# An mLSTM and ternary feed-forward layer: the opening's gates in one group, two value units of sequence 1 moved, two sums on another engine

## The reference

```python
x = x + mlstm(layernorm(x), Wq, Wk, Wv, Wog, Wig, big, Wfg, bfg, gamma, Wout)
x = x + ffn(layernorm(x), w1, b1, w2, b2)

# mlstm, 8 heads, key width 32, value width 64; i and f: gate rows (8 x 512 each)
i, f = 15*tanh((x @ Wig.T + big)/15), 15*tanh((x @ Wfg.T + bfg)/15)
# per step: m = max(logsig(f)+m, i); C = F*C + I*k v^T; n = F*n + I*k
# h = (q C) / (max(|q n|, exp(-m)) + eps); norm per head * gamma
# out = (sigmoid(x @ Wog.T) * h) @ Wout.T

# ffn: w1q, w2q = sign(w) * (|w| >= 0.7*mean|w|)      (2048 wide)
# out = gelu(x @ w1q.T + b1) @ w2q.T + b2
```

## Time and profile before

| | us |
|---|---|
| median of 3 runs | 1740.55 (1740.52 to 1741.01) |
| the profiled execution | 1742.3 |
| its span in the profile | 1740.6 |
| TensorE busy | 1707.5 (98%) |
| VectorE busy | 1437.6 (83%) |
| ScalarE busy | 1059.6 (61%) |

### The profile page before, as it was taken

One profiled execution on the slowest core, in us unless ns is written; L12 is line 12 of the kernel. 1 busy time (PEld: TensorE's weight loads), 2 busy tenths in 40 slices (PEclk: granted clock), 3 DMA queues, 4 the chain that ended last, 5 costly groups with the idle time before them and its releaser, 6 DMA issues.

```text
span 1740.6 us, 31380 instructions
## 1 busy us (share of the span) xinstructions
PE 1707.5 (98%) x12028; PEld 841.4 (48%) x12028; DVE 1437.6 (83%) x2528; ACT 1059.6 (61%) x1769; POOL 606.6 (35%) x477
## 2 busy tenths in 40 slices
PE   6899999999999999999999999999999999999999
PEld 4554445444444444445444444444444444454455
DVE  7888788897888978789887888988789788886872
ACT  6978375473746638375573746648375573847643
POOL 1242514335241442514235241442514235241430
PEclk9999999999999999999999999999999999999999
DMA  8736253442725326253442725336262442625120
GB/s 321 219 89 167 58 141 72 117 120 56 170 60 127 87 80 160 58 154 59 120 117 56 171 60 126 87 92 152 55 161 61 110 119 56 148 59 132 33 55 25
DMA packets 294981, 187.45 MB, mean 108 GB/s; under 512 B 239136, under 2 KB 260640, under 8 KB 289712
## 3 DMA queue, kind: packets, MB, share of 16 engines
q1 hardware_dynamic: 293248, 182.30, 41.7%
q10 hardware_dynamic: 1584, 3.15, 0.5%
HBM read 96.47 MB, written 20.23 MB: 67 GB/s over the span
## 4 chain that ended last, share of the span: by engine, by line
PE 81%; DVE 8%; DMA 3%; SPq 3%; issue 2%; POOL 1%; ACT 1%; POOLq 0%; DVEq 0%; ACTq 0%
PE pf L2073 24%; PE pf L2057 22%; PE pa L1926 17%; PE pa L1902 7%; PE psh L1926 5%; SPq L530 2%; PE psh L2013 2%; DMA kT<-shared 1%; PE psh L1968 1%; PE psh L2047 1%; DVE gT L1633 1%; PE pa L2013 1%; DVE dec L1482 1%; PE pa L1893 1%; PE psh L2009 1%
## 5 line engine op out<-in xcount | busy, mean ns | idle before, releaser
L2073 PE MATMUL pf<-w2T,gT 128*128 128x512 f16 x2048 | 505.8, 379 | 0.0
L2057 PE MATMUL pf<-x2T,w1T 128*128 128x512 f16 x1920 | 422.0, 379 | 0.0
L2057 PEld LDWEIGHTS pf<-x2T,w1T 128*128 128x128 f16 x1920 | 185.4, 98 | 222.5
L2073 PEld LDWEIGHTS pf<-w2T,gT 128*128 128x128 f16 x2048 | 195.5, 97 | 177.0
L1633 DVE SCALAR_TENSOR_TENSOR gT<-g,wscale,gT 128x512 f16<-128x512 f32 x240 | 208.5, 871 | 22.5 <-ACT gT L1046 20.2
L1926 PE MATMUL pa<-wT,xT 128*128 128x512 f16 x960 | 212.8, 379 | 0.6 <-ACT sig L970 0.6
L1043 ACT ACTIVATE g<-pf,b1c 128x512 f32<-128x512 f32 x240 | 164.1, 684 | 72.5 <-PE pf L2057 56.6
L1046 ACT ACTIVATE gT<-g,wscale 128x512 f16<-128x512 f32 x240 | 173.3, 722 | 7.9
L1926 PE MATMUL pa<-wT,shared 128*128 128x512 f16 x768 | 176.2, 379 | 1.6 <-DMA shared<-qT 0.8
L1051 ACT ACTIVATE ktok<-kT 128x512 f32<-128x512 f32 x64 | 40.4, 631 | 216.4 <-DVE kT L1528 214.9
L1902 PE MATMUL pa<-xT,wT 128*128 128x512 f16 x768 | 171.4, 379 | 0.0
(11 more groups left out here) (246 smaller groups left out, 2705.2 us busy)
## 6 DMA issues: line engine op xcount, KB each, us to landing
dec<-gate_r SPq DMA_DIRECT2D x32, 1024.0 KB, 6.1
xin<-L_attn_x SPq DMA_DIRECT2D x16, 1024.0 KB, 6.0
out<-x1b SPq DMA_DIRECT2D x64, 256.0 KB, 2.3
xres<-L_attn_x SPq DMA_DIRECT2D x16, 512.0 KB, 4.3
xres<-L_attn_x SPq DMA_DIRECT2D x32, 256.0 KB, 3.0
qw<-gate_w SPq DMA_DIRECT2D x128, 48.0 KB, 2.0
s<-state_w SPq DMA_DIRECT2D x60, 97.5 KB, 2.4
qw<-kT SPq DMA_DIRECT2D x120, 48.0 KB, 2.0
```

Source lines behind the costliest of these rows:

```text
L2057: last = nc.tensor.matmul(bank, w1T[:, k, tok(f)], x2T[:, part, :, k, :], start=(k == 0 and part == HI), stop=(k == KD - 1 and part == LO))
L2073: last = nc.tensor.matmul(bank, gT[:, part, f, tok(t)], w2T[:, f, :], start=(f == 0 and part == HI), stop=(f == NF - 1 and part == LO), sk ...
```

## The change

Everything that changes is in the first 135 us of the run.

- ScalarE loads its table by a small square at the very start; the squares of the query and key weights go behind the value and gate weights.
- The transposes and sums of `maxima` are parted, so that other work can stand between them.
- The gates of sequence 0 go to one column group (`first_gates`): all twelve matmuls add into the same 32 rows. ScalarE takes tanh directly from the bank, then the absolute value, then the exponential (`first_exponents`); the copy and the three additions are gone for this sequence. On VectorE the gate weights' lower part comes before two of the value weights, and the logarithm's steps stand apart (`gate_one`, `gate_rest`), ahead of `sequence(0)`.
- ScalarE's w2 sums: 0 ahead of tanh, 1 behind it, 2 and 3 behind the keys (before: 0, 1 and 2 ahead of tanh, 3 behind the keys).
- The w1 sums of pairs 2 and 3 become one reduction on VectorE (`absolute_sums(1)`), between `norm_apply(1)` and `chunk_decay(0)`.
- Two of the query weights' transposes go behind value tile 0 on TensorE.
- Value tile 1 of sequence 1 goes to the second bank of `pf`, in the place of 18 idle matmuls, of which 5 stay; ScalarE reads it between ternary pairs (pair 9 is taken earlier). Tiles 2 and 3 go ahead of projections 2 and 3 of sequence 0.

```diff
 s_dchain = sem("s_dchain")
+s_table = sem("s_table")
 s_sums = sem("s_sums")
...
 s_wfree = [sem(f"s_wfree{n}") for n in range(6)]
-s_abs = sem("s_abs")
+s_abs, s_abs_dve = sem("s_abs"), sem("s_abs_dve")
 s_asum = sem("s_asum")
...
-    sums = Chain(0, 4 + UNITS // 2)
+    sums = Chain(0, 4 + UNITS // 2 - 2)
...
+        act.wait_ge(gate_dve, at(b, 4, 0))
+        nc.scalar.activation(ge, ge, ACT.Exp).then_inc(gate_act, 1)
+    def gate_log(b):
         act.wait_ge(gate_dve, at(b, 4, 1))
-        nc.scalar.activation(ge, ge, ACT.Exp).then_inc(gate_act, 1)
-    def gate_log(b):
+        nc.scalar.activation(gl, gu, ACT.Ln).then_inc(gate_act, 1)
+    def gate_floor(b):
         act.wait_ge(gate_dve, at(b, 4, 2))
-        nc.scalar.activation(gl, gu, ACT.Ln).then_inc(gate_act, 1)
-    def gate_floor(b):
+        nc.scalar.activation(stack[32:32 + NH, :], gu, ACT.Exp, scale=-1.0).then_inc(gate_act, 1)
+    def late_decays(b):
         act.wait_ge(gate_dve, at(b, 4, 3))
-        nc.scalar.activation(stack[32:32 + NH, :], gu, ACT.Exp, scale=-1.0).then_inc(gate_act, 1)
-    def late_decays(b):
-        act.wait_ge(gate_dve, at(b, 4, 4))
         if b > 0:
...
         gate_log(b)
-        value(b, 1)
+        if not (isinstance(b, int) and b == 1):
+            value(b, 1)
         value(b, 2)
...
+    def first_exponents():
+        bank = pa_bank(0, U_GATE)
+        act.wait_ge(pa_fill, pa_filled(0, U_GATE))
+        nc.scalar.activation(th, pa[0:GROWS, bank, :], ACT.Tanh, bias=gate_bias[:, 0:1],
+                             scale=evac[0:GROWS, W_GATE:W_GATE + 1]).then_inc(tanh_ok, 1)
+        act.wait_ge(tanh_ok, 1)
+        nc.scalar.activation(ge, th[0:NH, :], ACT.Abs).then_inc(pa_free[bank], 1)
+        act.wait_ge(pa_free[bank], pa_done(0, U_GATE))
+        nc.scalar.activation(ge, ge, ACT.Exp, scale=-CAP).then_inc(gate_act, 1)
     def opening():
-        gate_copy(0)
-        absolute_sums2(1, 2)
-        gate_tanh(0)
+        absolute_sums2(0)
+        first_exponents()
+        absolute_sums2(1)
         value(0, 0)
-        gate_exp(0)
-        absolute_sums1(6, early=True)
+        gate_log(0)
         weights_hi(*USES_QK[0:3])
...
         weights_hi(USES_QK[3])
-        gate_log(0)
+        replace_rows(G_QK)
+        absolute_sums1(6, early=True)
         value(0, 2)
-        replace_rows(G_QK)
         weights_hi(*USES_O[0:2])
+        gate_floor(0)
         value(0, 3)
-        gate_floor(0)
         act.wait_ge(s_abs, sums.n)
...
         keys(0, 1)
-        absolute_sums2(3)
         weights_hi(USES_O[3])
+        absolute_sums2(2)
         replace_rows(G_O)
...
         gate_columns(0)
-        absolute_sums1(7, 0)
+        absolute_sums2(3)
         queries(0, 1)
-        absolute_sums1(1, 2, 3)
+        absolute_sums1(7, 0, 1)
         output_gate(0, 0)
...
             act.wait_ge(ps_fill, at(b, PS_FILLS, F_V + 1))
-            bank, free = ps[:, 1, :], ps_free[1]
+            bank, free = pf[:, 1, :] if isinstance(b, int) and b == 1 else ps[:, 1, :], ps_free[1]
         else:
...
             small2_gone(12)
+            ternary_out(9)
         squares(b, 2)
...
         if not run_f:
-            ternary_out(9)
+            value(1, 1)
             small2_gone(13)
...
+    act.wait_ge(s_pchain, 1)
+    nc.scalar.activation(hinv[:, :], half[:, :], ACT.Square).then_inc(s_table, 1)
     sum_squares(G_V)
     sum_squares(None)
-    sum_squares(G_QK)
     split_hi(*range(KD))
...
     replace_rows(G_V)
-    absolute_sums2(0)
+    sum_squares(G_QK)
     sequence(0, None, True)
...
-    def bounds(cols, step):
+    def row_maxima(step):
...
                                 ALU.mult).then_inc(s_rowmax, 1)
+    def bounds(cols, step):
+        known = PEAK_COLS[step - 1]
+        n = known.stop - known.start
         dve.wait_ge(s_allmax, step)
...
+    def absolute_sums(n):
+        dve.wait_ge(s_w12[0][n], 16)
+        nc.vector.tensor_reduce(asum1[:, 2 * n:2 * n + 2],
+                                rows[:, 4 * n:4 * n + 4, :].rearrange("p (n u) d -> p n (u d)", u=2), AX.X, ALU.add,
+                                apply_absolute_value=True).then_inc(s_abs_dve, 1)
     def thresholds():
-        dve.wait_ge(s_abs, 4 + UNITS // 2)
+        dve.wait_ge(s_abs, 4 + UNITS // 2 - 2)
+        dve.wait_ge(s_abs_dve, 1)
         nc.vector.tensor_reduce(asums[:, 0:1], asum1[:, :], AX.X, ALU.add)
...
         bank = pa_bank(b, U_GATE)
-        dve.wait_ge(gate_lo, at(b, 1, 1))
+        dve.wait_ge(gate_lo, at(b, 1, 0))
         nc.vector.tensor_tensor(th, pa[2 * QUAD:2 * QUAD + GROWS, bank, :], th, ALU.add).then_inc(gate_part, 1)
-        dve.wait_ge(gate_part, at(b, 2, 1))
+        dve.wait_ge(gate_part, at(b, 2, -1))
         nc.vector.tensor_tensor(th, pa[QUAD:QUAD + GROWS, bank, :], th, ALU.add).then_inc(gate_part, 1)
-        dve.wait_ge(gate_part, at(b, 2, 2))
+        dve.wait_ge(gate_part, at(b, 2, 0))
         nc.vector.tensor_tensor(th, pa[0:GROWS, bank, :], th, ALU.add).then_inc(pa_free[bank], 1)
...
         nc.vector.tensor_scalar(ge, th[0:NH, :], CAP, None, ALU.mult).then_inc(gate_arg, 1)
-        dve.wait_ge(gate_arg, at(b, 3, 1))
+        dve.wait_ge(gate_arg, at(b, 3, 0))
         nc.vector.scalar_tensor_tensor(ge, ge, -1.0, ge, ALU.mult, ALU.min).then_inc(gate_dve, 1)
+    def first_floor():
+        dve.wait_ge(tanh_ok, 1)
+        nc.vector.tensor_scalar(gf, th[0:NH, :], CAP, 0.0, ALU.mult, ALU.min)
     def gate_logs(b):
...
         nc.vector.tensor_scalar(gf, th[0:NH, :], CAP, 0.0, ALU.mult, ALU.min)
-        if b == 0:
-            scales(LATER, 2)
+        gate_one(b)
+        gate_rest(b)
+    def gate_one(b):
...
         nc.vector.tensor_scalar(gu, ge, 1.0, None, ALU.add).then_inc(gate_dve, 1)
-        if b == 0:
-            weights_lo(USES_QK[0])
-        dve.wait_ge(gate_dve, at(b, 4, 2))
+    def gate_rest(b):
+        dve.wait_ge(gate_dve, at(b, 4, 1))
         nc.vector.scalar_tensor_tensor(ge, gu, 1.0, ge, ALU.subtract, ALU.subtract).then_inc(gate_arg, 1)
-        dve.wait_ge(gate_arg, at(b, 3, 2))
+        dve.wait_ge(gate_arg, at(b, 3, 1))
         nc.vector.tensor_tensor(gf, gf, ge, ALU.add).then_inc(gate_arg, 1)
...
-        if b == 0:
-            gate_minus(b)
-            gate_logs(b)
-            weights_lo(*USES_QK[1:4])
         dve.wait_ge(i_loaded, at(b, 16, 16))
         nc.vector.tensor_scalar(gi, gi, CAP, None, ALU.mult)
-        dve.wait_ge(gate_arg, at(b, 3, 3))
+        dve.wait_ge(gate_arg, at(b, 3, 2))
         dve.wait_ge(gate_act, at(b, 5, 2))
...
             norm_apply(b + 1, range(T))
+            absolute_sums(1)
             chunk_decay(b)
...
     norm_apply(0, range(T))
+    row_maxima(1)
     bounds(EARLY, 1)
...
     split_lo(2, 3)
-    weights_lo(*USES_V)
+    weights_lo(*USES_V[0:2])
     weights_lo(USE_GATE)
+    weights_lo(*USES_V[2:4])
     largest()
-    gate_sum(0)
+    first_floor()
+    row_maxima(2)
+    gate_one(0)
     bounds(LATER, 2)
+    gate_rest(0)
+    scales(LATER, 2)
+    weights_lo(*USES_QK)
     sequence(0, None, True)
...
-    def maxima(sums, peak_count, step):
+    def peak_transpose(sums, peak_count, step):
...
         nc.tensor.transpose(peak_rows[0:n, :], peak[:, known], ident[:, :]).then_inc(s_rows, 1)
+    def peak_sums(step):
+        n = PEAK_COLS[step - 1].stop - PEAK_COLS[step - 1].start
         pe.wait_ge(s_rowmax, step)
...
             pe.wait_ge(xT_loaded, at(b, 16, -16))
+    def first_gates():
+        bank = take_pa(0, U_GATE)
+        for k in range(KD):
+            for n, (ws, xs) in enumerate(PARTS):
+                last = nc.tensor.matmul(bank[0:QUAD, :], wgT[:, k, ws, :], xT[:, xs, :, k, :],
+                                        start=(k == 0 and n == 0), stop=(k == KD - 1 and n == 2))
+        last.then_inc(pa_fill, 1)
...
             opening()
-        else:
+        elif not (isinstance(b, int) and b == 1):
             late_values(b, 2)
...
         weights_ready(USE_GATE)
-        gates(0)
-        weights(*USES_QK[0:2])
+        first_gates()
         weights_ready(*USES_V)
         tokens(0, U_V, xT[:, :, 0, :, :], C_V)
-        maxima(3, 1, 2)
-        weights(USES_QK[2])
+        peak_transpose(3, 1, 2)
+        weights(USES_QK[0])
+        peak_sums(2)
+        weights(*USES_QK[1:3])
         late_values(0, 1)
...
         weights_out(2, 3)
-        busy_until(10, 18)
+        pe.wait_ge(pf_free[0], 5)
+        keep_busy(pf[:, 0, :], 5)
+        x_ready(1)
+        pe.wait_ge(ps_free[1], at(1, PS_USES[1], 0))
+        pe.wait_ge(pf_free[1], 5)
+        token_products(pf[:, 1, :], xT[:, :, 1, :, :], C_V).then_inc(ps_fill, 1)
+        ternary_transpose(10)
+        pe.wait_ge(ps_free[1], at(1, PS_USES[1], 1))
         ternary_transpose(11)
...
         ternary_transpose(13)
-        x_ready(1)
         gates(1)
...
         ternary_transpose(15)
-        late_values(1, 1)
         tokens(1, U_V, xT[:, :, 0, :, :], C_V)
+        late_values(1, 2)
+        late_values(1, 3)
         project(0, 2)
```

(11 more changed lines are left out.)

## The result

The changed kernel takes 1744.03 us (median of 20 runs, 1741.64 to 1747.01), the kernel before 1740.53 (20 runs, 1739.36 to 1741.91): ratio 1.0021, 95% interval 1.0014 to 1.0027. It is slower, by 3.5 us where 1.65 was forecast, and outside the range (1737.3 to 1743.6). Its runs also spread more: standard deviation 1.57 us against 0.63. Its profiled execution took 1741.64, the shortest of its runs, and that of before 1742.3, above all 20 of its timed runs. The two spans (1739.9 and 1740.6) rank the kernels the wrong way round, so the stretches have to be compared. Up to the first feed-forward use of sequence 1 (144.75 before, 145.53 after) the changed kernel is 0.78 us later. From there to the end it is 1595.9 us before and 1594.4 after; over all 18 traces of this document this rest takes 1594.1 to 1596.6 us, so it differs between executions by more than the change is worth.

A forecast was written before the change was run, and what follows sets the result against it. TensorE, 98% busy, was taken as the bound. Opening 0, VectorE sum and order +0.2, projection 3 +1.83, old slack -0.38 gave +1.65 us on 1740.55: 1742.2 us; 8-in-10 range 1737.3 to 1743.6.

The forecast's parts named there:

- Items 1 and 2: Opening: earlier tanh and one gate group; gate matmuls at 20.9, V0 at 25.5, first keys about 0.6 us later.
- Item 3: Opening: keys 0.6 us late are hidden in TensorE's 1.14 us wait at 46.06 for a lower weight part.
- Item 4: Opening: gate rows, issued earlier, still queue behind sequence 1's x and land at 39.2 to 39.5; gain 0.
- Item 5: Opening: the w1 reduction moved to VectorE delays chunk decays, thresholds and ternary products by 0.2 us.
- The handover order: Sequence 0 to 1: keys start 3.35 us earlier, but projection 3 ends 1.83 us later, delaying work that waits for it.
- All three waits: Handover: TensorE idles ahead of sequence 1's first query, gate transposes and second query, using up the 3.35 us.
- The full gain: Rival: keys start 3.35 us earlier and nothing behind stops TensorE, giving 1737.2 us; chance 0.17.
- the cancelling: Rival: projection 3's lateness costs only 0.25 at the gate transposes, giving 1740.8; chance 0.18 together with gate rows passing the loads.
- the end of the fourth score product: Behind the handover: it ends at 157.9, before TensorE wants the bank at 158.6, so its lateness hides.
- the 3.35 us are waited away in three places, and TensorE goes on 1.65 us later: Handover: three waits consume the earlier keys; the second query starts at 133.45 instead of 131.80.

The follow-up runs named there:

- e2: The change's opening alone (gates in one group, sums moved), with the handover of the kernel before: 1741.27 us, ratio 1.0006.
- e6: Changed kernel with value 0, projections 2 and 3, then values 2 and 3; ScalarE reads value 0 ahead of the gate's exponential: 1740.67 us.
- e9: e2 with five idle matmuls ahead of the transposes of the last output-gate weights: 1740.50 us, ratio 1.0002.
- e5: Changed kernel with 7, 5 and 4 idle matmuls in its three waits of sequence 1: 1742.68 us, ratio 1.0014.
- e11: Changed kernel with the idle matmuls of both e5 and e9: 1742.21 us, ratio 1.0013.
- e1: Changed kernel run again with no edit: 1743.74 us, ratio 1.0019.
- e3: The change's handover alone, with the opening and sums of the kernel before: 1743.34 us, ratio 1.0016.
- e4: Changed kernel with value tile 3 of sequence 1 moved behind projection 3 of sequence 0: 1741.06 us, ratio 1.0004.
- e13: e11 with the thresholds ahead of the decay columns on VectorE: 1743.85 us, ratio 1.0019.
- e12: Changed opening with the idle matmuls of e9, handover order of e6, key 1 read ahead of the last tokens' upper part: 1740.76 us, ratio 1.0005.

## Why the prediction was wrong, point by point

- **Items 1 and 2 (gates, tanh): right.** Gates at 20.90 for a forecast 20.9, V0 at 25.61 for 25.5, tanh at 25.71 for "near 26".
- **Item 3 (keys 0.6 late, hidden): wrong sign, and the cover was misread.** I counted from one trace. In the first trace of the changed kernel the keys are 0.29 late (39.43 for 39.14). Over the traces the gates start at 19.5 to 20.9 in the changed opening and at 22.1 to 22.8 in the old one, and the first keys at 37.4 to 39.4 for 39.1 to 40.4. TensorE is earlier, while the release of the last output gate weights hangs on the gate rows, which land at 38.5 to 40.5 whether they are issued at 24.5 or at 30.9. So the wait at 46 us does not shrink. It is 0 to 1.1 us in the traces with the old opening and 0 to 4.0 with the new one; in two of seven traces without idle matmuls there (e2, e6) the clock fell. Filling it was worth 0.48 us of the opening alone (e2 to e9) and 0.33 of the changed kernel (e5 to e11), each against its own runs of before; neither is clear of noise by itself.
- **Item 4 (gate rows held by the load of x): right in the main, not in the detail.** Landed at 38.77 and used at 38.79, forecast 39.2 to 39.5; over the other traces with both forms of opening used at 38.5 to 40.6, never near 28. But they do not always land behind all of x: in the changed kernel's trace the last part of x lands at 39.59, 0.8 us after them. In 11 of the 18 traces they come 0.2 to 1.0 ahead of that part, in seven, before's among them, 0.2 to 0.3 behind it.
- **Item 5 (VectorE sum, +0.2): size near, cause missed.** The decay copy was at 59.13, 20.34 behind the gate rows' use, for 20.29 in the trace of before; but in the others with the old opening it is 19.5 to 20.2, as the decay rows land. The sum fixes it at the late end: the decay columns come straight behind it, GpSimd's product with them, and the threshold step, 0.9 us into the product, always meets it. Before, some executions missed it in part or whole. Mean distance of the five old traces 65.53, of the new 65.9: +0.4 us. That the sum is what fixes it is read from the traces; moving it back alone was not tried.
- **The handover order: right.** All three waits came, in the places named and for the reasons named, 1.83, 1.26 and 1.13 us. Keys at 119.81 (forecast 120.43); they follow projection 3, which so ends 1.84 us later from the same start than before (forecast 1.83); and the second query is 1.40 us later from the same start, for 1.83 - 0.38 = 1.45. The full gain and the cancelling are refuted: the query never started early in this order. One sum is off without effect: the end of the fourth score product, 155.73 + 0.68 + 2.03 - 0.8, is 157.6 and not 157.9; it ended at 157.2, and TensorE did not wait for it.
- **The step that failed: "the 3.35 us are waited away in three places, and TensorE goes on 1.65 us later".** I priced the 4.2 us of waiting at their length alone and put what they do to the clock at nothing, without a reason: the uses behind them stand in the sum at full clock, as the earlier trace rows have them. In e1, e3 and e4 the clock fell to 0.50 in them, and the query behind took 4.23 to 4.45 us for 2.76: +1.5 where it happens. By medians it is 0.9 of the changed kernel (e1 to e5, each against its own runs of before), at the edge of the noise; the rows at 0.50 in three traces, and their absence in e5, carry it. The same term was missing in item 3. The lateness itself was sized right, 1.40 for 1.45.

The Trainium skill, "TensorE: Matmul & The Clock Gate", section "What's actually happening", says that the cold stretch varies from run to run of one kernel. The traces agree: the same waits left the clock at 1.00 in one execution and took it to 0.50 in the next (e1), and the spread fell from 1.02 to 0.49 us once both places were filled (filling the handover alone left it at 1.06).

The Trainium skill, "SBUF — State Buffer", section "SBUF: two separate sides", says that a VectorE instruction in a 2-port performance mode, or with two inputs in SBUF (then only against a GpSimd instruction that reads SBUF), and a GpSimd instruction exclude each other from a shared port pair: the one that starts first holds it for its whole length, and the other is blocked. The traces agree as far as they go. The last threshold step ends 0.02 to 0.03 us behind GpSimd's 1.81 us product in all fourteen traces in which the product still has 0.2 us or more to run when the step starts, while the reciprocal inside the same product takes its usual 0.17. In e13, where a ternary step starts first, it is the product that is longer, by 0.44. Which steps are in a 2-port mode no trace shows.

The sum, against the 3.3 us of e1: handover 1.4, its clock 0.9, the opening's clock 0.3 to 0.5, the threshold step 0.4, together 3.0 to 3.2. Of these the first is read from traces; the second and third are differences of medians with a trace beside each; the fourth is a mean over traces, and no run took it back. e11, without the clock terms, is 2.1 over before for 1.8. The last 0.1 to 0.3 is open; it is inside the intervals, and TensorE's small waits for VectorE at the scores of sequence 1 (0.40 in e5, none in e11) may be part of it.

## What to carry to other kernels

A wait on a full TensorE has two prices: its length, and the clock that it can cost the work behind it. When an order of work is changed so that several waits come close together, ask for both, put idle matmuls in them, and take a wider spread of the runs as a hint, not a proof, that the second is being paid in some of them (e12 spread by 1.08 us though its trace kept the clock). An earlier start ahead of a release that is fixed by something else only makes the wait longer.

## What was not expected of the hardware

- One execution's trace can be the luckiest or the unluckiest of its kernel: before's profiled 1742.3 lay above its 20 timed runs, after's 1741.64 at the bottom of them.
- A 128x2 step on VectorE took 0.91 us for 0.17 beside a GpSimd product, while another 128x2 step just ahead of it, beside the same product, took its 0.17; and two steps of 128x1024 took 2.97 for 1.42.
- A 16 KB copy issued 3.6 us earlier landed 0.7 us earlier: 12.26 us under way for 9.34, behind 1 MB loads in the same queue, and 0.8 us ahead of the last part of one of them.
